# Cross-attention scores computed in both orientations, with the row maximum as extra rows, in place of turned probabilities

## What is computed

```
x = layernorm(x + self_attention(x))       # 16 heads of 128, 2 key heads, rotation, softcap, causal
x = layernorm(x + cross_attention(x, ctx)) # 16 heads of 16, 256 context keys, an additive mask
x = layernorm(x + network(x))              # a router picks 4 of 16 blocks; hidden width 1024, GELU

# cross_attention, the part that the change is about
q = w8a8_linear(x, wq, bq)                 # x and wq rounded to 8-bit steps by their row maximum
k, v = cond @ wk.T + bk, cond @ wv.T + bv
scores = einsum('bhnd,bhld->bhnl', q, k) * inv_sqrt_d + mask
attn = softmax(scores)                     # over the 256 keys
o = einsum('bhnl,bhld->bhnd', attn, v)
return w8a8_linear(o, wo, bo)
```

## Time and profile before

| | |
|---|---|
| median of 3 executions | 386.93 us (385.92 to 387.41) |
| span of the profiled execution, first to last instruction | 382.7 us |
| TensorE (PE) busy | 370.5 us, 97% |
| VectorE (DVE) busy | 293.5 us, 77% |
| ScalarE (ACT) busy | 233.6 us, 61% |
| GpSimd (POOL) busy | 151.0 us, 39% |

### The profile page before, as it was taken

One profiled execution on the slowest core, in us unless ns is written; L12 is line 12 of the kernel. 1 busy time (PEld: TensorE's weight loads), 2 busy tenths in 40 slices (PEclk: granted clock), 3 DMA queues, 4 the chain that ended last, 5 costly groups with the idle time before them and its releaser, 6 DMA issues.

```text
span 382.7 us, 8976 instructions
## 1 busy us (share of the span) xinstructions
PE 370.5 (97%) x3038; PEld 315.8 (82%) x3038; DVE 293.5 (77%) x900; ACT 233.6 (61%) x494; POOL 151.0 (39%) x172
## 2 busy tenths in 40 slices
PE   8999999999999999999999999999999998999894
PEld 7678897978889888787998787989887897778783
DVE  2999888865688487899888868887878888976443
ACT  1658655545576865465686863867794455995240
POOL 4697947457544414454432332441302530000111
PEclk9999999999999999999999999999999999999999
DMA  8991753653524243124344221121121200000000
GB/s 283 367 345 57 249 174 75 189 169 84 166 84 109 88 137 113 46 75 155 111 109 140 57 57 40 47 82 57 45 82 48 79 2 2 15 16 2 0 30 27
DMA packets 21404, 38.42 MB, mean 100 GB/s; under 512 B 2544, under 2 KB 12144, under 8 KB 21360
## 3 DMA queue, kind: packets, MB, share of 16 engines
q1 hardware_dynamic: 20544, 37.06, 31.4%
q10 hardware_dynamic: 816, 0.79, 0.6%
HBM read 25.52 MB, written 5.24 MB: 80 GB/s over the span
## 4 chain that ended last, share of the span: by engine, by line
PE 80%; DVE 10%; issue 3%; DMA 3%; POOL 2%; ACT 1%; SPq 0%; POOLq 0%; DVEq 0%; ACTq 0%
PE acc L595 10%; PE bank L489 10%; PE bank L680 8%; PE bank L562 6%; PE bank L741 6%; PE bank L761 6%; PE bank L539 5%; PE bank L692 4%; PE bank L669 3%; PE bank L565 3%; PE bank L576 3%; PE bank L547 3%; PE bank L621 2%; PE bank L658 2%; PE bank L508 2%
## 5 line engine op out<-in xcount | busy, mean ns | idle before, releaser
L918 ACT ACTIVATE xs<-xs,xneg 128x256 f32<-128x256 f32 x128 | 53.5, 499 | 13.2 <-DVE xneg L1197 13.2
L1362 POOL TENSOR_TENSOR q_T<-q_T,rope_s 128x512 f32<-128x512 f32 x24 | 31.7, 1323 | 63.1 <-DMA rope_s<-rope_t 58.0
L1373 POOL TENSOR_TENSOR a_lo<-a_flat,a_hi 128x512 fp32r<-128x512 f32 x32 | 42.7, 1336 | 22.6 <-ACT a_flat L838 22.6
L595 PE MATMUL acc<-wo_s,a_hi 128*128 128x256 f32 x256 | 50.6, 296 | 0.0
L1197 DVE CUSTOM_DVE_ANT_0 xs<-bank,mask_s 128x256 f32<-128x256 f32 x128 | 45.7, 419 | 5.0 <-PE bank L669 4.6
L1391 POOL TENSOR_TENSOR small<-small,half 128x1 f32<-128x1 f32 x24 | 13.9, 584 | 75.9 <-DVE small L1081 75.9
L562 PE MATMUL bank<-v_s,p_near 128*128 128x129 f32 x256 | 42.0, 277 | 0.9 <-POOL p_near L1380 0.6
L595 PEld LDWEIGHTS acc<-wo_s,a_hi 128*128 128x128 f32 x256 | 39.4, 189 | 2.6 <-issue 2.6
L562 PEld LDWEIGHTS bank<-v_s,p_near 128*128 128x128 f32 x256 | 35.4, 191 | 5.1 <-issue 3.8
L489 PE MATMUL bank<-x_hi,wqkv_hi 128*128 128x256 f32 x124 | 38.6, 311 | 0.0
L595 PE MATMUL acc<-wo_s,a_lo 128*128 128x256 f32 x128 | 35.9, 280 | 0.0
(11 more groups left out here) (168 smaller groups left out, 970.1 us busy)
## 6 DMA issues: line engine op xcount, KB each, us to landing
wo_s<-wo_parts SPq DMA_DIRECT2D x24, 512.0 KB, 3.3
rope_s<-rope_t SPq DMA_DIRECT2D x54, 128.0 KB, 2.3
wo_parts<-wo_s SPq DMA_DIRECT2D x8, 512.0 KB, 3.3
xs<-in_wo SPq DMA_DIRECT2D x8, 256.0 KB, 5.8
stage<-in_wqkv SPq DMA_DIRECT2D x2, 512.0 KB, 5.1
xp_T<-in_wqkv SPq DMA_DIRECT2D x2, 512.0 KB, 6.9
y<-in_x SPq DMA_DIRECT2D x4, 256.0 KB, 3.1
ctx_s<-in_ctxT SPq DMA_DIRECT2D x4, 256.0 KB, 3.1
```

Of the source, the lines that this page charges most:

```text
L595: ins = mm(acc[:, t, :], a[x], wo_s[:, slot, w, m, :], start=(j == 0 and t == 0 and m == 0 and p == 0), stop=(j == PAIRS - 1 and m == 1 an ...
L918: activation(xs[:, t, m, m2, :], xs[:, t, m, m2, :], ACT.Exp, bias=xneg[:, t, m, m2:m2 + 1], scale=-1.0)\
L1362: g.tensor_tensor(dst, dst, (rope_s if b else rope_t)[:, n % 2], ALU.add).then_inc(sig["rotated", 0], 1)
L1373: g.tensor_tensor(a_lo[:, j % 2], a_flat[:, j % 2], a_hi[:, j % 2].bitcast(F32), ALU.subtract)\
```

## The change

The queries and keys are no longer interleaved on VectorE. Their rows are ordered on the host so that after one transpose (queries) or none (keys, made as [channel, key] by `ctx_k`) a high and a low part of all heads stand in `part_hi` and `part_lo`, each [128, 2, 256]. Six transfers in each batch (`send_k`) stack them in `kS` and six (`send_q`) in `qS`, two heads on 96 rows, with zeros in the other head's rows of `qS`. `xscore` gives [query, key] on 96 rows as before but only for the row maximum: what the instruction writes beside `xneg` is not used. `turn_n` turns the negated maxima of eight heads, `send_n` puts their high and low parts into rows 96 and 97 of `qS`, where `kS` holds ones. `xprob` multiplies again, [key, query] on 98 rows, so that its result already has the maximum taken off; VectorE adds a turned mask (`maskT_s`), ScalarE takes the exponential over 512 columns at a time, and `xmix` uses it directly on 256 columns. `turn_p`, `turn_k`, and both copies to `xp_T` are gone. Both query tiles now go through each step together, in one stream `x`; the small operations of the norms and of `quantise` cover both tiles. `clear` sets `kS` and `qS` once on GpSimd. `ORDER` is a new string.

The plan (the old functions are printed above; the first and the last two lines of the new string are shown):

```diff
+    prep += [("clear", 0, 0, 0)] if b == 0 else []
+    return [*prep, ("ctx_k", b, 0, 0), ("ctx_v", b, 0, 0), ("send_k", b, 0, 0)]
+
+
+def cross_ops(b):
+
+    ops = [("quant_x", 0), ("turn_x", 0), ("query", 0), ("turn_q", 0), ("send_q", 0)]
+    for half in range(2):
+        ops += [("xscore", j) for j in range(4 * half, 4 * half + 4)] + [("turn_n", half), ("send_n", half)]
     for g in range(QUADS):
-        ops += [("turn_p", 2 * g), ("turn_p", 2 * g + 1)]
-        if g + 1 < QUADS:
-            ops.append(("xscore", g + 1))
-        if g + 2 < QUADS:
-            ops.append(("turn_q", g + 2))
-        ops.append(("xmix", g))
-    ops += [("turn_o", 0), ("quant_o", 0), ("turn_ox", 0), ("outproj", 0), ("scale2", 0)]
-    return [(kind, b, i, t) for kind, i in ops]
+        ops += [("xprob", 2 * g), ("xprob", 2 * g + 1)]
+        if g:
+            ops.append(("xmix", g - 1))
+    ops.append(("xmix", QUADS - 1))
+    ops = [(kind, b, i, 0) for kind, i in ops] + [("turn_o", b, 0, t) for t in range(TT)]
+    return ops + [(kind, b, 0, 0) for kind in ("quant_o", "turn_ox", "outproj", "scale2")]
...
+    "rrrrrrrsrssrmsmmscmsmmrrmmsmrmmmrsscrmmmcmmsmmmmmmrsmmsmmmrcmmmcmcmmccmcmrmcmmrrcmmmsrscsmxrrmxsmxmmxrmmm"
...
+    "nnmxsrssxmmxxxrnmxxxmxsxmxmmmmxxxmxonsxxmxmxxxxxnsoxxommxxmxmmmmmxmmxmmxmcmxcxcxxnxnxnxxxonnxxxxnxxnxxxxx"
+    "xxxxxxxxxxxxnxxxonnnnnononnnnnnonnnonooo")
```

SyncE:

```diff
+            def send_k(b):
+
+                wait_for(sp, "k_lo", b, 1)
+                wait_filled(sp, "xprob", b - 1, XPAIRS - 1, 0, 1)
+                for m in range(2):
+                    for part, src in enumerate((part_hi, part_lo, part_hi)):
+                        r0 = 3 * XD * m + XD * part
+                        sp.dma_start(kS[r0:r0 + XD].bitcast(F32), src[:, m, :]).then_inc(k_in, 16)
+
+            def send_q(b):
+
+                if b == 0:
+                    sp.wait_ge(cleared, 2)
+                wait_for(sp, "q_lo", b, 1)
+                wait_filled(sp, "xprob", b - 1, XPAIRS - 1, 0, 1)
+                for m in range(2):
+                    for part, src in enumerate((part_hi, part_hi, part_lo)):
+                        r0 = 3 * XD * m + XD * part
+                        sp.dma_start(qS[r0:r0 + XD, :, m, :].bitcast(F32), src[:, m, :]).then_inc(q_in, 16)
+
+            def send_n(b, half):
+
+                wait_for(sp, "n_lo", b, half)
+                wait_filled(sp, "xprob", b - 1, XPAIRS - 1, 0, 1)
+                js = slice(4 * half, 4 * half + 4)
+                for row, src in enumerate((part_hi, part_lo)):
+                    r0 = XROWS + row
+                    sp.dma_start(qS[r0:r0 + 1, js].rearrange("p j m n -> p (j m) n").bitcast(F32), src[0:XPAIRS, half, :])\
+                        .then_inc(n_in[half], 16)
```

TensorE:

```diff
+            def xscore(b, j):
+
+                if j == 0:
+                    pe.wait_ge(k_in, 96 * (b + 1))
+                    pe.wait_ge(q_in, 96 * (b + 1))
+                for t in range(TT):
+                    ps = claim("xscore", b, j, 0, t)
                     for m in range(2):
+                        ins = mm(ps[:, m * T:(m + 1) * T], qS[0:XROWS, j, m, t * P:(t + 1) * P], kS[0:XROWS, j, :],
+                                 start=True, stop=True)
+                    ins.then_inc(filled, 1)
+
+            def turn_n(b, half):
+
+                ps = claim("turn_n", b, half)
+                wait_for(pe, "xmax", b, 16 * half + 15)
+                for t in range(TT):
+                    ins = transpose(ps[0:XPAIRS, t * P:(t + 1) * P], xneg[:, t, half * XPAIRS:(half + 1) * XPAIRS], ident_s[:])
+                ins.then_inc(filled, 1)
+
+            def xprob(b, j):
+
+                if j % 4 == 0:
+                    pe.wait_ge(n_in[j // 4], 32 * (b + 1))
+                    if b == 0:
+                        pe.wait_ge(cleared, 2)
+                for k in range(TT):
+                    ps = claim("xprob", b, j, 0, k)
+                    mm(ps[:, :], kS[0:XSHIFT, j, k * P:(k + 1) * P], qS[0:XSHIFT, j].rearrange("p m n -> p (m n)"),
+                       start=True, stop=True).then_inc(filled, 1)
+
+            def xmix(b, g):
+
+                ps = claim("xmix", b, g)
+                wait_for(pe, "xv", b)
+                wait_for(pe, "xexp", b, 4 * g + 3)
                 for k in range(TT):
                     for h in range(4):
-                        ins = mm(ps[XW * h:XW * (h + 1), 0:P], xv_s[:, k, 4 * g + h, :], xp_T[:, t, h % 2, h // 2, k, :],
+                        ins = mm(ps[XW * h:XW * (h + 1), 0:T], xv_s[:, k, 4 * g + h, :], xe[g % 2][:, h // 2, k, h % 2, :],
                                  start=(k == 0), stop=(k == TT - 1))
                 ins.then_inc(filled, 1)
```

ScalarE, which in place of `xexp` and the copies of `turn_p` has:

```diff
+            def xprob(b, j):
+
+                for k in range(TT):
+                    wait_for(act, "xsum", b, 2 * j + k)
+                    p = xe[j // 2 % 2][:, j % 2, k].rearrange("p m q -> p (m q)")
+                    activation(p, p, ACT.Exp).then_inc(sig["xexp", 0], 1)
```

VectorE:

```diff
+            def rest_of(kind, b, c, hi, lo):
+
+                wait_for(dve, hi, b, 1)
+                for m in range(2):
+                    v.scalar_tensor_tensor(part_lo[:, m, :].bitcast(F32R), bank(kind, b)[:, m * T:(m + 1) * T],
+                                           bias_c[:, c, m:m + 1], part_hi[:, m, :], ALU.add, ALU.subtract)\
+                        .then_inc(sig[lo, 0], 1)
...
+            def xscore(b, j):
+
+                if j == 0:
                     dve.wait_ge(mask_in, 16 * (b + 1))
+                    wait_filled(dve, "turn_x", b)
+                if j % 4 == 0:
+                    wait_filled(dve, "turn_n", b - 1, j // 4)
+                for t in range(TT):
+                    wait_filled(dve, "xscore", b, j, 0, t)
+                    for m in range(2):
+                        h = 2 * j + m
+                        if 2 * t + h >= 2:
+                            wait_for(dve, "xmax", b, 4 * j + 2 * t + m - 2)
+                        v.tensor_tensor_reduce(out=q_int[:, m, :], in0=bank("xscore", b, j, 0, t)[:, m * T:(m + 1) * T],
+                                               in1=mask_s[:, t, :], scale=-1.0, scalar=3.0e38, op0=ALU.add,
+                                               op1=ALU.min, accum_out=xneg[:, t, h:h + 1]).then_inc(sig["xmax", 0], 1)
+
+            def turn_n(b, half):
+
+                wait_for(dve, "n_hi", b, half)
+                v.tensor_tensor(part_lo[0:XPAIRS, half, :].bitcast(F32R), bank("turn_n", b, half)[0:XPAIRS, 0:T],
+                                part_hi[0:XPAIRS, half, :], ALU.subtract).then_inc(sig["n_lo", 0], 1)
+
+            def xprob(b, j):
+
+                if j == 0:
+                    dve.wait_ge(maskT_in, 16 * (b + 1))
+                if b == 0 and j == 2:
+                    dve.wait_ge(w1_lo_done, WPARTS)
+                if j % 2 == 0:
+                    wait_filled(dve, "xmix", *((b, j // 2 - 2) if j >= 4 else (b - 1, j // 2 + 2)))
+                for k in range(TT):
+                    wait_filled(dve, "xprob", b, j, 0, k)
+                    v.tensor_tensor(xe[j // 2 % 2][:, j % 2, k],
+                                    bank("xprob", b, j, 0, k)[:].rearrange("p (m q) -> p m q", m=2),
+                                    maskT_s[:, k, :].unsqueeze(1).to_broadcast([P, 2, T]), ALU.add)\
+                        .then_inc(sig["xsum", 0], 1)
```

GpSimd:

```diff
+            def clear():
+
+                g.memset(kS[:].rearrange("p j n -> p (j n)").bitcast(F32), 1.0).then_inc(cleared, 1)
+                g.memset(qS[:].rearrange("p j m n -> p (j m n)").bitcast(F32), 0.0).then_inc(cleared, 1)
```

530 lines of the change are left out of this document (253 added, 277 removed).

## The result

The changed kernel takes **422.1 us** (median of 4 runs, 420.0 to 425.2) where the kernel before took 386.4 beside it: 1.095 times as long, 95% interval 1.089 to 1.101. The profiled execution has a span of 418.2 us against 379.0 in the forecast and 382.7 before. The forecast (383.2, range 374 to 394) missed, in sign and in size.

The account below looks back on a forecast made before the run. The prediction took TensorE, busy 97%, as the bound. It summed 299.3 us to the last `proj`, 55.8 of batch 3's chain, 2.0 for clock and 21.9 for the last network to 379.0, plus 4.2 outside: 383.2 us, range 374 to 394.

Parts of the forecast that it names:

- The step that failed: Before the last `proj`: TensorE's waits for transfers, VectorE's bank releases and `clear` add 2.2 us idle together (0 to 8).
- The transfers' term: Six stacking transfers, from the rests to the stacked operand: 5.3 us (4.6 to 7.1), priced from the half swap's row.
- The work: TensorE's work: 92 transposes go in each batch, other products change; −6.5 us a batch, −26 in all.
- Scores for the maximum: TensorE, 32 instructions a batch on 96 rows: 0.12 us each in place of 0.103, taken as +0.9 us a batch.
- `xprob`: TensorE, 16 new products of 512 columns a batch: 0.23 us each, +3.7 (up to +7.3 at the float32 price).
- `xmix`: TensorE, 128 instructions of 128 columns become 64 of 256: −0.5 us in each batch.
- The body: Up to the end of the last `proj`: 299.3 us, from 306.7 − 19.5 + 13.5 − 3.6 + 2.2.
- three signs of being wrong: `near` or `mix` wait for swaps in batches 1 to 3; 98-row product at float32 price; tail's clock row reads 0.5.
- The tail: Behind the last `proj`: 17.4 us to batch 3's first row minimum, 38.4 to the last network, 2.0 for low clock.
- Costs put at nothing: GpSimd's `clear` (about 5.6 us, covered), VectorE's net −1.6 us and ScalarE's drop of about 12 us a batch: each 0.
- SP's queue holds the rotation: Rival, chance 0.23: stacking holds SP 3.5 us twice a batch, swaps behind wait, 10.5 us more idle: 393.7 us.
- The clock stays low: Rival, chance 0.07: from batch 3's first score to the last network TensorE runs at 1.2 GHz, +17 us: 398.

Follow-up runs that it names:

- e16: Changed kernel in its given order, each stacking transfer writing every sixth partition instead of 16 neighbouring ones; 1.0634 times the kernel before.
- e12: Changed kernel in a third order, batch 3's tokens in the buffer of its transposed input, 53 unused products of constants in the tail; 1.0162 times the kernel before.
- e4: Changed kernel with one of the six stacking transfers for keys and one for queries, scores not the reference's; 1.0477 times the kernel before.
- e1: Changed kernel with the old order up to the first cross step of batch 0; 416.6 us against 383.2 for the kernel before, some 1.087.
- e11: Changed kernel in a third order found by search, batch 3's tokens in the buffer of its transposed input; 1.0199 times the kernel before.
- e14: Kernel before, its own operations, in an order found the same way as the changed kernel's third order; 1.0166 times the kernel before as given.
- e3: Changed kernel with half of the stacking transfers issued from ScalarE's queue instead of SP's; 1.0925 times the kernel before.
- e13: Changed kernel in its given order with all stacking transfers of keys and queries issued from ScalarE's queue instead of SP's; 1.1404 times the kernel before.
- e2: Changed kernel with unused products of constants in TensorE's gaps in batch 3's cross-attention; 1.0930 times the kernel before.

## Why the prediction was wrong

**The step that failed** is one sentence: "Every such place, the claims of banks that VectorE must release, and `clear` get 2.2 us of new idle time together (0 to 8)." It was 20.3 us (23.9 of idle time before the last `proj`, less the 3.6 of before): 9.0 at `turn`, 5.0 at `xscore` 0 of batches 0 to 2, 3.8 at `mix`, the rest in small waits. I had counted the steps between `turn_q` and `xscore` 0 and called them cover, "closely". I didn't lay VectorE's queue beside TensorE's in batch 0 (`quant_w`: 9.0 us of waits at `turn`), and took the transfers for six issues with one landing behind them.

**The transfers' term** was 5.3 us (4.6 to 7.1), from a row in which each transfer of a swap writes 64 partitions (not 128, as e16's expectation has it) and lands in 2.3. The measured set takes 8.4, above the range; with its rows spread (e16) the wait is 2.8 us shorter, so most of the 3.1 us is the 16 neighbouring partitions of each. And I priced only who waits for the set, not what it does to the transfers beside it: the swaps' 5.6 us.

**The work** was nearly right. Price by price, groups of e12, whose clock is at the upper level (0.99 over the span); L819 are the products of constants:

```profile
L703 PE MATMUL bank<-kS,qS 96*128 96x256 f32 x128 | 21.5, 306 | 1.2 <-issue 1.1
L723 PE MATMUL bank<-qS,kS 98*128 98x512 f32 x64 | 20.2, 425 | 0.0
...
L819 PE MATMUL acc<-ones 128*128 128x128 f32 x106 | 13.2, 277 | 0.0
...
L733 PE MATMUL bank<-xs,xv_s 128*32 128x256 f32 x128 | 8.6, 385 | 0.6 <-ACT xs L983 0.6
L733 PE MATMUL bank<-xp_T,xv_s 128*32 128x256 f32 x128 | 8.5, 384 | 0.0
```

- Scores for the maximum: 21.5 against 13.2, +8.3 in four batches, forecast +3.6. The forecast set 0.12, a distance of two starts, against 0.103, a group's busy time over its count. The distance was right, 0.12 at the median in e12, and against it stand 0.09 in the mean before, so by distances the change is 128 × 0.03 = +3.8. Busy time also holds the end of each product that no other overlaps, and here VectorE's minima, 0.34 us apart, set the pace.
- `xprob`: 20.2 for 64, forecast 14.8, by the same mixing: the distance of two starts is 0.235 at the median in e12, as forecast (0.22 to 0.24), and not the float32 price.
- `xmix`: 17.1 against 18.2, −1.1, forecast −2.
- The sum's range in each batch is −1.6 to −8.2 by its own terms, not −2.5 to −8.5; nothing hangs on it.
- In all: e12 is busy 362.1 (sum of its windows), less 13.2 it is 348.9, against 370.5: −21.6 us, forecast −26.

**The body**, then: 26.7 us late, of which 18.1 are idle time beyond the 5.8 that the forecast had (3.6 and 2.2), and 8.6 are longer busy time: an estimated 5 to 6 for the half clock behind the gaps, and the remainder for work that was saved less than thought. By the experiments the transfers have most of the idle time at 97, 109, 188 and 276 us (gone in e4), the order of batch 0 that at 22 to 54 us (gone in e1). How much each would cost alone isn't settled, for e1 shows that they hide each other. Two of the three signs of being wrong that the prediction named came true: `mix` waits for swaps, and the tail's clock reads 0.5.

**The tail.** To the first row minimum 24.9 us for 17.4: 3.1 for the transfers; the second norm's scaling of batch 2 stands ahead of `norm1` and waits for GpSimd's root, so `norm1` starts 1.8 us behind the last `proj` and not 0.1; one quantising operation (L1163) of 1.37 us for 0.43 while GpSimd adds the bias, 0.9; the rest is half clock and small waits. From there to `turn_z` 42.6 for 38.4 and the 2.0 for the clock. The forecast had said that TensorE would idle some 23 us there and that the saving of batch 3 would be lost. That was right: it idles 22.5 of the 67.5 us. e11 against e14 shows it in a better order too: of 16.7 us of saved work, 13.4 come back as idle time behind the last `proj` and 6.4 before it.

**Costs put at nothing.** `clear` was covered: GpSimd takes 5.3 us for it (5.6 forecast), and no wait of TensorE ends on it. The cover was the order's: in e1 TensorE waits 3.0 us for a rest that stands behind it. VectorE's work stayed the same, 293.8 us against 293.5. ScalarE dropped by 39 us, and no run shows that this brought time.

**The rivals.** "SP's queue holds the rotation" saw the right victims, `near` and `mix` in batch 1, and the right sign, but its mechanism fell for the most part with e3 and e13 (at most 1.1 of the 3.8 us at `mix` went with the queue), and its 393.7 was 28 short. "The clock stays low" was true in the tail (0.50 for 24 us), but cost 3.9 us by e2, not 17: TensorE was busy only 12.6 of those 24 us and waited for others in the rest. The weight that "TensorE waited 3.6 us in 306.7" got as evidence was too great: it showed how well the old order fitted the old operations, and said nothing on a new order with new ones.

## What to carry to other kernels

When a change saves work on the engine that is 97% busy, price the waits of the new order, not only its work: lay the queue of the second engine beside the first one's for each batch, and ask of each new transfer how many partitions it writes and which transfers run beside it. A saving in the body that lengthens the last batch's chain can be lost again, as that chain stands in no other batch's shade. And compare two versions under orders found the same way, or the order is what was measured.
